# Layer-norm statistics taken tile by tile in the stage before, in a six-stage transformer kernel on one core

## The reference

```python
x = x + 0.5 * L0_ffn(layernorm(x))     # stage 0: linear layer + low-rank experts, soft mask
x = x + L0_attn(layernorm(x))          # stage 1: 32 heads of 16, causal, plus an adapter prefix
x = x + 0.5 * L0_ffn(layernorm(x))     # stage 2: as stage 0
x = x + 0.5 * L1_ffn(layernorm(x))     # stage 3: 16 experts, top 2, plus a shared expert
x = x + L1_attn(layernorm(x))          # stage 4: 32 query heads of 128 on 8 key/value heads
x = x + 0.5 * L1_ffn(layernorm(x))     # stage 5: as stage 3
def layernorm(x):                      # eps = 1e-5
    return (x - mean(x)) / sqrt(var(x) + eps)
```

## Time and profile before

| | |
|---|---|
| median of three runs | 1803.34 us |
| the profiled execution's own time | 1799.84 us |
| its span | 1798.1 us |
| PE busy | 1606.9 us (89%) |
| DVE busy | 1004.5 us (56%) |
| ACT busy | 900.9 us (50%) |
| POOL busy | 984.8 us (55%) |

### The profile page before, as it was taken

One profiled execution on the slowest core, in us unless ns is written; L12 is line 12 of the kernel. 1 busy time (PEld: TensorE's weight loads), 2 busy tenths in 40 slices (PEclk: granted clock), 3 DMA queues, 4 the chain that ended last, 5 costly groups with the idle time before them and its releaser, 6 DMA issues. The chain is left out here.

```text
span 1798.1 us, 26487 instructions
## 1 busy us (share of the span) xinstructions
PE 1606.9 (89%) x8164; PEld 1242.7 (69%) x8164; DVE 1004.5 (56%) x2630; ACT 900.9 (50%) x1876; POOL 984.8 (55%) x1122
## 2 busy tenths in 40 slices
PE   5597899998768998589999999999999999979996
PEld 4486555546547886467878788787878778757884
DVE  5561556551657236655656565656565656665235
ACT  3112565652221231477777776777677777731230
POOL 2252555541221443378787877777878777812533
PEclk9798789988879999899999999999999999989999
DMA  2200000000134933244544353444434344463834
GB/s 85 91 10 3 2 3 2 3 3 1 37 141 154 339 133 111 85 107 108 115 111 114 82 136 89 107 108 103 122 91 127 81 100 89 91 229 121 318 119 139
DMA packets 312096, 180.24 MB, mean 100 GB/s; under 512 B 281895, under 2 KB 283767, under 8 KB 309568
## 3 DMA queue, kind: packets, MB, share of 16 engines
q1 hardware_dynamic: 300160, 152.81, 30.5%
q0 software_dynamic: 11840, 26.25, 4.7%
HBM read 111.08 MB, written 22.54 MB: 74 GB/s over the span
## 5 line engine op out<-in xcount | busy, mean ns | idle before, releaser
L1325 POOL TENSOR_TENSOR st_prob<-st_prob,st_rinv 128x512 f32<-128x512 f32 x256 | 266.3, 1040 | 177.0 <-DVE st_rinv L1393 177.0
L1329 POOL TENSOR_TENSOR st_plane<-st_prob,st_plane 128x512 f16<-128x512 f32 x256 | 307.6, 1211 | 0.3 <-ACT st_plane L1245 0.3
L1245 ACT ACTIVATE st_plane<-st_prob 128x512 f16<-128x512 f32 x256 | 161.2, 630 | 126.9 <-POOL st_prob L1325 126.8
L1261 ACT ACTIVATE st_prob<-st_score,st_nmax 128x512 f32<-128x512 f32 x256 | 175.2, 685 | 59.8 <-DVE st_nmax L1400 57.2
L1400 DVE TENSOR_REDUCE st_nmax<-st_score 128x1 f32<-128x512 f32 x256 | 175.1, 684 | 41.5 <-PE st_score L108 38.6
L2038 DVE CUSTOM_DVE_ANT_0 st1b_dump<-st1b_score,st1b_maskrow 128x128 f32<-128x128 f32 (+3 forms) x256 | 112.7, 487 | 95.5 <-PE st1b_score L1736 68.9
L1240 ACT ACTIVATE st_pthi<-st_plane_t 128x512 fp32r<-128x512 f16 x256 | 159.5, 623 | 3.4 <-DMA st_plane_t<-st_plane 3.2
L1370 DVE CAST st_ptlo<-st_plane_t 128x512 fp32r<-128x512 f16 x256 | 148.9, 582 | 2.6 <-DMA st_plane_t<-st_plane 2.6
L1374 DVE TENSOR_TENSOR st_olo<-st_outp,st_ohi 128x512 fp32r<-128x512 f32 x64 | 44.2, 690 | 166.8 <-ACT st_ohi L1249 166.8
L1893 ACT ACTIVATE st1b_slabs<-st1b_across 128x512 f32<-128x512 f32 (+1 forms) x192 | 90.6, 526 | 90.4 <-PE st1b_across L1755 70.1
L106 PE MATMUL st_outp<-st_pthi,st_vhi 128*128 128x512 f32 x256 | 103.8, 406 | 28.4 <-ACT st_pthi L1240 27.4
(11 more groups left out here) (380 smaller groups left out, 4056.3 us busy)
## 6 DMA issues: line engine op xcount, KB each, us to landing
st_raw<-in_moe_w SPq DMA_DIRECT2D x40, 768.0 KB, 7.3
sorted_outs<-st_ln_xn SPq DMA_DIRECT2D x62, 256.0 KB, 4.1
st_qraw<-in_gqa_q SPq DMA_DIRECT2D x8, 1024.0 KB, 5.4
st_oraw<-in_gqa_o SPq DMA_DIRECT2D x8, 1024.0 KB, 5.3
rows<-st_ln_xn SPq DMA_DIRECT2D x2, 2048.0 KB, 9.3
st_kvraw<-in_gqa_kv SPq DMA_DIRECT2D x8, 512.0 KB, 3.9
st_plane_t<-st_plane SPq DMA_TRANSPOSE x256, 2.7
st1a_raw<-in_w_attn SPq DMA_DIRECT2D x3, 1024.0 KB, 6.6
```

The source lines that it names most:

```text
L1245: act.activation(plane[t][:, 0:T], prob[:, t, :], ACT.Copy).then_inc(upper_ready, 1)
L1261: act.activation(prob[:, t, :], score[t][:, :], ACT.Exp, bias=nmax[:, slot:slot + 1], accum_out=rsum[:, slot:slot + 1]).then_inc(exp_ready, 1)
L1325: pool.tensor_tensor(prob[:, t, :], prob[:, t, :], rinv[:, slot:slot + 1].broadcast_to([P, T]), ALU.mult).then_inc(norm_ready, 1)
L1329: pool.tensor_tensor(plane[t][:, T:2 * T], prob[:, t, :], plane[t][:, 0:T], ALU.subtract).then_inc(lower_ready, 1)
```

## The change

`load_stage` is gone. The class `Moments` holds what was the first part of `Norm`: `take(t)` is the `bn_stats` of tile `t`, `close()` the eight `bn_aggr`, `root_table` a square root of 16 columns of the identity into a buffer that nobody reads, so that ScalarE's function table is that of the root. `stats`, `mv` and `table` are now allocated once for the whole kernel (192, 64 and 64 bytes per partition), ahead of the stages' buffers.

Stage 0 loads `x` itself, in eight DMAs with a semaphore each, with the identity behind them, and takes each tile's statistics as it lands. Every stage but the last takes the statistics of the tiles that it finishes, between its adds, closes them and calls `root_table`, all before its barrier. The next `Norm` starts at `ve`.

ScalarE now does the root first in stages 0, 2, 3 and 5, too. In stages 0 and 2 it does the first four `xhi` ahead of the weights' splits and the last four behind them, and PE's transposes wait for one copy into `aw`, not for three.

```diff
-def load_stage(nc, env, dram):
...
-                sp.dma_start(env["ident"][:, :], dram["ident"]).then_inc(loaded, 16)
-                sp.dma_start(env["x"][:, :, :], dram["x"].rearrange("(t p) c -> p t c", p=P)).then_inc(loaded, 16)
-                sp.wait_ge(loaded, 32)
+class Moments:
+    def __init__(self, s, env):
+        self.x, self.stats, self.mv = env["x"], env["stats"], env["mv"]
+        self.stats_ready, self.mv_ready = s.sem("stats_ready"), s.sem("mv_ready")
+        self.table, self.ident = env["table"], env["ident"]
+
+    def take(self, dve, t):
+        dve.bn_stats(self.stats[:, t, :], self.x[:, t, :]).then_inc(self.stats_ready, 1)
+
+    def close(self, dve):
+        dve.wait_ge(self.stats_ready, NT)
+        for t in range(NT):
+            dve.bn_aggr(self.mv[:, t, :], self.stats[:, t, :]).then_inc(self.mv_ready, 1)
+        dve.wait_ge(self.mv_ready, NT)
+
+    def root_table(self, act):
+        act.activation(self.table[:, :], self.ident[:, 0:16], ACT.Sqrt)
...
 # class Norm, vector_rows
-        for t in range(NT):
-            dve.bn_stats(self.stats[:, t, :], x[:, t, :]).then_inc(self.stats_ready, 1)
-        for t in range(NT):
-            dve.wait_ge(self.stats_ready, t + 1)
-            dve.bn_aggr(mv[:, t, :], self.stats[:, t, :]).then_inc(self.mv_ready, 1)
-        dve.wait_ge(self.mv_ready, NT)
         dve.tensor_scalar(ve[:, :], mv[:, :, 1], 1e-5, None, ALU.add).then_inc(self.var_ready, 1)
...
 # lime_ffn_stage, sync
+                if first:
+                    for t in range(NT):
+                        sp.dma_start(x[:, t, :], dram["x"][t * P:(t + 1) * P, :]).then_inc(x_loaded[t], 16)
+                    sp.dma_start(ident[:, :], dram["ident"]).then_inc(ident_loaded, 16)
...
 # tensor
-                pe.wait_ge(aw_ready, 3)
+                pe.wait_ge(aw_ready, 1)
+                if first:
+                    pe.wait_ge(ident_loaded, 16)
...
 # scalar
+                if first:
+                    act.wait_ge(ident_loaded, 16)
+                    entry.root_table(act)
+                norm.scalar_std(act)
                 act.wait_ge(al_ready, 1)
...
-                norm.scalar_std(act)
+                norm.scalar_hi(act, 0, KC)
...
-                norm.scalar_hi(act)
+                norm.scalar_hi(act, KC)
...
+                moments.root_table(act)
...
 # vector, its start and its last loop
+                if first:
+                    for t in range(NT):
+                        dve.wait_ge(x_loaded[t], 16)
+                        entry.take(dve, t)
+                    entry.close(dve)
...
                                              op0=ALU.mult, op1=ALU.add).then_inc(x_added, 1)
+                    if j >= 1:
+                        dve.wait_ge(x_added, j)
+                        moments.take(dve, order[j - 1])
+                dve.wait_ge(x_added, NT)
+                moments.take(dve, order[NT - 1])
+                moments.close(dve)
...
 # moe_stage, scalar and the end of vector
+                norm.scalar_std(act)
                 wait(act, g_loaded, 16)
                 act.activation(ghi[:, :, :], gw[:, :, :], ACT.Copy).then_inc(ghi_ready, 1)
-                norm.scalar_std(act)
...
-                add_step(NI - 1)
-                combine(2 * NT)
+                if last_stage:
+                    add_step(NI - 1)
+                    combine(2 * NT)
+                else:
+                    combine(2 * NT)
+                    for t in range(TB):
+                        add_step(NI - 1, 1)
+                        wait(dve, *written[t])
+                        moments.take(dve, t)
+                    for t in range(TB, NT):
+                        wait(dve, *written[t])
+                        moments.take(dve, t)
+                    moments.close(dve)
...
 # gqa_stage, the end of vector
                     turned_lo(LAST, NU - 1, t)
+                wait(dve, o_added, outs(KV1, 1))
+                for t in range(TB):
+                    moments.take(dve, t)
                 out_lo(LAST, NU - 1)
                 for u in range(1, 5):
                     add(KV1, u, score[u - 1])
+                    if u >= 2:
+                        wait(dve, o_added, outs(KV1, u))
+                        moments.take(dve, TB + u - 2)
+                wait(dve, o_added, outs(KV1, 5))
+                moments.take(dve, NT - 1)
+                moments.close(dve)
...
 # projection_block, vector
                     dve.tensor_tensor(x[:, t, :], bank[t % 4][:, :], x[:, t, :], ALU.add).then_inc(added, 1)
+                    if t >= 1:
+                        dve.wait_ge(added, t)
+                        moments.take(dve, t - 1)
+                dve.wait_ge(added, NT)
+                moments.take(dve, NT - 1)
+                moments.close(dve)
...
 # macaron_kernel
+        env["stats"], env["mv"] = s.sb("stats", [P, NT, 6]), s.sb("mv", [P, NT, 2])
+        env["table"] = s.sb("table", [P, 16])
...
-        load_stage(nc, env, dram)
```

More of the change, by code:

```diff
@@ L139, in __init__ @@
         self.rows = rows
-        self.stats_ready, self.mv_ready, self.var_ready, self.std_ready = (s.sem(n) for n in ("ln_stats_ready", "ln_mv_ready", "ln_var_ready", "ln_std_ready"))
+        self.var_ready, self.std_ready = s.sem("ln_var_ready"), s.sem("ln_std_ready")
         self.rstd_step, self.xn_ready, self.turned_ready = (s.sem(n) for n in ("ln_rstd_step", "ln_xn_ready", "ln_turned_ready"))
@@ L176, in scalar_std, with scalar_hi @@
         act.activation(self.sd[:, :], self.ve[:, :], ACT.Sqrt).then_inc(self.std_ready, 1)
-    def scalar_hi(self, act):
-        for n, (h, k) in enumerate(self.order):
+    def scalar_hi(self, act, first=0, end=None):
+        for n, (h, k) in list(enumerate(self.order))[first:end]:
             act.wait_ge(self.turned_ready, n + 1)
@@ L213, in lime_ffn_stage @@
         bank = [s.ps(f"bank{n}", [P, 512]) for n in range(8)]
-        norm = Norm(s, env, bank)
+        first = name == "st0"
+        norm, moments = Norm(s, env, bank), Moments(s, env)
+        if first:
+            entry, ident_loaded, x_loaded = Moments(Stage(nc, ctx, "entry"), env), s.sem("ident_loaded"), [s.sem(f"x_loaded{n}") for n in range(NT)]
         w_loaded, a_loaded, c_loaded = s.sem("w_loaded"), s.sem("a_loaded"), s.sem("c_loaded")
@@ L472, in moe_stage @@
         bank = [s.ps(f"bank{n}", [P, 512]) for n in range(8)]
-        norm = Norm(s, env, bank)
+        norm, moments, last_stage = Norm(s, env, bank), Moments(s, env), name == "st5"
         yb, yg = [norm.xn[:, n, :] for n in range(3)], [norm.xn[:, n, :] for n in range(3, NT)]
@@ L728, in _ @@
                         act_hi(i)
+                if not last_stage:
+                    moments.root_table(act)
             @block.gpsimd
@@ L2121, in _ @@
                     last.then_inc(out_ready, 1)
+            @block.scalar
+            def _(act):
+                moments.root_table(act)
             @block.vector
```

4 lines of the change are left out of this document (3 added, 1 removed).

## The result

The changed kernel is slower. Its median is 1810.74 us (1798.87 to 1816.86, 18 runs) against 1801.95 us (1795.53 to 1809.81, 18 runs) for the kernel before, a ratio of 1.0048 with a 95% interval of 1.0034 to 1.0063. The forecast was 1783. The profiled execution after spans 1808.5 us, before 1798.1.

A forecast was written before the change was run, and what follows sets the result against it. It took PE as fullest, with DVE alone setting the six stage openings' end. Part 1's 13.6 us and part 2's 6.7 gave 20.3 off a median of 1803.3, so 1783; range 1778 to 1789, or 1776 to 1793 with A.

The forecast's parts named there:

- Part 1: Tails of the stages and stage 0's load: statistics taken there bring the six first rows forward, 13.6 us in all.
- The load terms: Stages 1 and 4: an earlier barrier starts the loads earlier, so the first product gains 1.7 us each beyond Part 1.
- Part 2: Starts of stages 0, 2, 1 and 4: POOL's subtraction moves off DVE's rows and loads start earlier, 6.7 us in all.
- Gain 2.4 in stage 0 ... +15.3, gain 1.9: Wide product in stages 0 and 2 starts sooner after the first row, at +15.3 in stage 2 for +17.2 before.
- POOL's bias adds and routing as a collision: Stages 0 and 2, behind the wide product's start: bias adds meet DVE's small routing operations, 0.5 us lost in each.
- 4.3 - 1.0: Stages 0 and 2: gain from ScalarE's early first four xhi, 2.4 + 1.9 us, less 1.0 for POOL's bias adds.
- The 320 bytes ahead of the stages' buffers: Shifted addresses of the stages' buffers: costed at nothing, with 2 us allowed either way.
- Nothing inside the stages is touched: Premise: only the openings and the tails of the stages before them gain or lose, the whole 20.3 us.
- A: Rival: Part 2 doesn't come, collision changes place or PE's clock stays lower for longer; gain 12, 1791 us, chance 0.16.
- B: Rival: weights' loads start later in stages 1 to 5 and decide each start; +11 us, 1814, chance 0.04.
- C: Rival: eight pieces of x load one after the other, last landing 17 us later; 1800 us, chance 0.03.
- The rule on shared ports: Two-port DVE tensor_scalar and GpSimd block each other; second half: one-SBUF-input DVE operations aren't touched, else up to 2.4 us per stage.

The follow-up runs named there:

- order192: pad192 with ScalarE rounding all eight x^T tiles behind the weights again in stages 0 and 2; 1786.65 us, ratio 0.9904 to the kernel before.
- pad192: The changed kernel with 192 unused bytes behind its 320, so later buffers stand 512 bytes above their old place; 1796.53 us, ratio 0.9976 to the kernel before.
- reduce192: pad192 with GpSimd's all-reduce of the peaks ahead of its eight bias adds in stages 0 and 2; 1784.08 us, ratio 0.9904 to the kernel before.
- congr: reduce192 with the gqa stage's small buffers last, so pthi, ptlo, ohi, olo stand at 128 modulo 512; 1782.03 us, ratio 0.9867 to the kernel before.
- beforemoving: The kernel before with only the gqa stage's buffers that PE streams on odd multiples of 64 bytes, laid out in another order; 1814.99 us, ratio 1.0058.

## Why the prediction was wrong

**Part 1, the statistics in the tails, was right in its mechanism and three quarters of its size.** Stage by stage it had the first row at 11.9 (12.91; the last piece of `x` landed at 10.0, the upper bound), and from the last adds' start 10.4 us to the first row of stage 1 (67.41 to 77.8) where 10.6 were measured (68.07 to 78.62). In stage 2 it had 3.7 us from the last add to the first row (454.87 to 458.6); it is 4.6 (454.74 to 459.35). In stages 3 and 5 it had 11.8 and 8.0 from the start of the last adds; 12.3 and 8.8. In stage 4 it had 10.7 from the last four adds' start, and it is 10.9. Some tenths are missing in each, most at the new barrier, where DVE's `ve` comes later than I took it. Measured between the same points before and after, the six gains are 4.0, 0.4, 3.3, 0.0, 0.5 and 2.0 us, 10.2 in all for the forecast 13.6. The load terms came: from first row to first product it is 10.7 us for 12.1 in stage 1 and 8.4 for 10.2 in stage 4, so 1.4 and 1.8 for 1.7 each. The experiment that leaves these two parts, order192, gains 16.1 us by its median for a forecast of 13.6 + 3.4.

**Part 2 had the right sum for the wrong chain.** Its step "Gain 2.4 in stage 0 ... +15.3, gain 1.9" is right to 0.1 us for the start of the wide product, but in stage 2 partly by luck: there the first product moves from +17.2 to +15.8 with the old order of ScalarE too, and of the 1.9 the early roundings give 0.5. What failed is the silent step behind it, that what starts earlier ends the stage earlier. The part names POOL's bias adds and routing as a collision worth 0.5 us each; it never asks what is queued on POOL behind them, the all-reduce with its 6 us, and who waits for it. That row was in the trace of before, with a wait of 2.20 us on DVE: a chain that DVE already waited for was left out of the count. Instead of gaining 4.3 - 1.0, the order of ScalarE costs 10 to 11.5 us.

**The addresses.** The term "The 320 bytes ahead of the stages' buffers I cost at nothing; no row shows an address, so I allow 2 us either way" measured 14.2 us. This is the largest term, and no row of the trace of before could give it. But the bound was chosen, not worked out: 0.5% on each of PE's products, in a kernel where PE is busy nine tenths of the time, is already 8 us. The sentence "Nothing inside the stages is touched", on which the whole sum stands, was false for the same reason, and the prediction's last paragraph names "the loops of stage 4 at another pace" as what would show it wrong. It did.

**The sum.** -16.1 (statistics, root and loads, order192 against before) + 9.9 (ScalarE's order, pad192 against order192) + 14.2 (addresses, changed kernel against pad192) = +8.0; measured +8.8. That the two agree proves nothing, since the three are steps of one path from the kernel before to the changed one; the 0.8 is the difference between two medians of the kernel before (1802.76 and 1801.95). What carries the split is that each step was also taken from another start: the addresses on the kernel before (16.7), the order on the unpadded kernel (11.5).

**The rivals.** A held that part 2 doesn't come, because a collision only changes place or PE's clock stays low for longer; something like the second is what happened, at more than its price, but in another gap: behind the wide product, not between transposes and first product. B, late loads, had the right sign and the wrong mechanism: in stages 1 and 4 the first product starts at 89.27 and 739.2, 1.1 and 0.3 us earlier than before. C: with eight pieces of `x` the last statistic starts at 10.01, where with one piece the first started at 10.03. The rule on shared ports that the prediction cites from the Trainium skill (SBUF — State Buffer, section Who interferes with whom) agrees with the traces in its second half, too: in stage 0 the last four `xlo` run beside `wlo` and take 2.48 us together, and the mean of all eight is 687 ns for 679 before.

## What to carry to other kernels

Where an operation is moved up on one engine, follow every chain that leaves the operations it passes, to the engine that waits with the least slack; a wait of 2 us on a side engine is 2 us of cover, not a proof that it's hidden. A new small buffer ahead of large ones is a change to every product: keep streamed operand and weights on the same place modulo 256 bytes, and pad what is added to a multiple of 256. When a profile shows several symptoms of one change (here slower transposes and slower products), move each by itself before naming one as the cause.

## What the hardware showed

- A product of 128x128 by 512 columns in fp32r is issued every 228.0 ns when streamed operand and weights are alike modulo 256 bytes, every 229.9 ns where the stream stands 64 above the weights, and every 232.6 to 232.8 ns where it stands 128 or 192 above them, with nothing else running (bench). The Trainium skill, SBUF — State Buffer, section Who interferes with whom, has two independent read ports for the two and says that PE never waits on anyone; the measurement shows that the pace of its products still depends on how the two operands' addresses stand to each other. By what mechanism is not shown.
- The DMA transposes land after 2.7 to 2.8 us where their buffers stand at 256 modulo 512 bytes, and after 3.1 where they stand at 64. No other place was read.
- The heads' part of stage 1 has no fixed time. reduce192 and congr are alike up to the gqa stage, yet from the first row of stage 1 to that of stage 2 one profile has 376.9 us and the other 385.2, with a granted clock of 0.86 and 0.81 from 130 to 280 us. Over the kernels here it goes from 377 to 390 (390.3 in beforemoving for 384.5 before, though nothing of stage 1 was edited). A comparison of two single profiles across such a stage is good to some 8 us, no better; what is found above rests on stretches beside it and on medians of 6 to 18 runs. Whether part of this difference belongs to the build, and so stays in a median, was not tried; differences of medians of a few us between two kernels are unsure by that much.
